# Attention by pairs of heads in one order with its neighbours, in a two-layer transformer block on one core

## The chip, the core and the metric

The kernel runs on one core of a Trainium2 chip. Its engines work side by side: TensorE (PE) multiplies into PSUM, eight banks of 512 columns; VectorE (DVE), ScalarE (ACT) and GpSimd (POOL) read and write SBUF, VectorE and ScalarE also PSUM; SyncE (SP) issues most transfers. The metric is the device time of one execution in microseconds (us). A difference is told as a per cent of the time before.

## What is computed

Four sub-layers on 2048 tokens of width 256, each with a residual and a layer norm behind it. The change touches the third (16-head causal attention, head width 16) and the seams to its neighbours:

```
x = _layernorm(x + _L0_attn_ref(x))
x = _layernorm(x + _L0_ffn_ref(x, ...))        # two experts of eight, low-rank parts
x = _layernorm(x + _L1_attn_ref(x, w_qkv, w_o))
x = _layernorm(x + _L1_ffn_ref(x, ...))        # mixture of 32 experts, top 8

# _L1_attn_ref, B = 1, S = 2048, 16 heads
q, k, v = split(x @ w_qkv.T)
scores = where(causal, q @ k.T / sqrt(16), min)
attn = softmax(scores) @ v
return attn @ w_o.T
```

## The kernel before

Every engine has its own program, written out in order; semaphores (`sig`, `sem`) join them. Tokens go in four blocks `b` (or `qb`) of 512 and 16 tiles of 128. A float32 product is made of three products of rounded parts, a high and a low one of each operand (`product`, `low`).

Attention works on four groups `g` of four heads. The queries and keys of a group stand in `stack`: per head 64 rows with the four combinations of parts, two rows for the maximum and padding up to 96 rows. Each score is computed twice. First **by query**, to find each query's maximum: a unit `(g, h, qt, kb)` is one head, one query tile and one block of keys, one product of 96 rows (L1390), on the diagonal a mask product behind it (L1393), and one VectorE reduction (L992) into `mpart`. There are 640 units; they take turns in PSUM banks 4 and 5, and a unit waits for the reduction two units back. When a round `(g, qb)` has its last unit, the maxima are reduced once more (L998), turned by TensorE (L1403), copied in two parts to `mrow` (L959, L743) and put by eight GpSimd transfers (L508) into the maximum rows of `stack`. Then **by key**: a step `(g, qb, kt)` takes one key tile against the 512 queries of the block for four heads (L1485, mask L1489), banks 0 to 3; ScalarE takes the exponentials of two heads at a time, 1024 wide (L680), and TensorE adds the values (L1447) into bank 6, for four heads in four column groups and in two halves of 256 queries. The sum of the exponentials comes with them, since the values have a column of ones. At a round's end VectorE copies bank 6 (L1027), TensorE turns it (L1503) and VectorE divides (L967, L969).

The order is set by `attention_plan`: 160 steps with 22 empty ones ahead (`lead`), and four units in every slot (`rate`). So a step's slot on TensorE holds unit, two heads, unit, two heads, unit, half of the last step's values, unit, the other half. Twelve of the empty slots are done among the queries and keys of blocks 2 and 3 (`early`). Ahead of attention stand, block by block, values, turning of the next block, queries and keys in four chunks, each written to `qk_dram` and loaded from there into `stack` by SP; GpSimd fills the padding rows (L555). In the last round's steps the output is turned and projected tile by tile for blocks 0 to 2 (`tail_turn`, `tail_tile`). Behind the last step come block 3's projection, the turning of `x` for the mixture, its logits, the gates, and then the 48 parts of the mixture, each 24 products for gates and ups and 24 for the way down.

```
lead, rate = 88, 4
steps = [None] * (lead // rate)
steps += [(g, qb, kt) for g in range(NG) for qb in range(NB) for kt in range(TPB * (qb + 1))]
return steps, [units[rate * s:rate * (s + 1)] for s in range(len(steps) + 4)], units
```

## Time and profile before

| | |
|---|---|
| median of 3 runs | 1653.36 us (1650.28 to 1655.07) |
| span of the profiled execution, first to last instruction | 1652.2 us |
| instructions in it | 22841 |

The profile gives the profiled execution as its span; no time of its own around the span is given. In its rows PE is TensorE's products, PEld its weight loads beside them. A group of instructions has its line, engine, operation, what it writes and reads, how many there are, busy time, mean time of one and the idle time of its engine ahead of it. A row of the timeline has start, length and what it is; "x3" behind it says that three were merged, and a length is then that of all. PEclk is the granted clock of TensorE, where 1.00 is 2.4 GHz and 0.50 is 1.2 GHz.

### The profile page before, as it was taken

What the parts mean: (1) busy time and instruction counts of PE and PEld (TensorE: products, weight loads), DVE (VectorE), ACT (ScalarE), POOL (GpSimd) and SP (SyncE); (2) the same over time, 40 slices, a digit from 0 to 9 for tenths busy, and PEclk for the clock granted to TensorE, in tenths of its full rate; (3) what the DMA queues carried; (4) which work ended last, traced back from release to release, by engine and by line L of the source; (5) the groups of instructions that cost most, each with busy time, mean ns of one, the idle gap of its engine ahead of it and who ended that gap; (6) DMA issues with size and microseconds to landing.
All of it is one profiled execution on the core that took longest, in us unless ns stands there. A gap on an engine that the chain in (4) does not pass through costs nothing.

```text
span 1652.2 us, 22841 instructions
## 1 busy us (share of the span) xinstructions
PE 1528.5 (93%) x9236; PEld 1130.4 (68%) x9236; DVE 998.6 (60%) x1864; ACT 616.6 (37%) x900; POOL 275.7 (17%) x282
## 2 busy tenths in 40 slices
PE   5699999999997689999999999999889999999994
PEld 4578788788786445555555555555678888888884
DVE  3555664746646666777777777773457444565444
ACT  3132422323323101455455455447423444444441
POOL 3220110200202132010011001001012222232220
PEclk9699999999999855899999999999979999999997
DMA  6000000000002558000800530100001111111110
GB/s 259 0 1 1 1 1 0 1 0 1 20 0 70 141 97 95 9 2 1 101 5 2 64 42 2 37 2 2 2 19 49 58 46 44 46 48 49 48 55 26
DMA packets 30329, 59.77 MB, mean 36 GB/s; under 512 B 7440, under 2 KB 14352, under 8 KB 28176
## 3 DMA queue, kind: packets, MB, share of 16 engines
q1 hardware_dynamic: 26128, 58.04, 16.0%
q8 instruction: 73, 1.20, 0.3%
q0 software_dynamic: 4096, 0.28, 0.3%
q14 instruction: 32, 0.26, 0.1%
HBM read 47.41 MB, written 10.49 MB: 35 GB/s over the span
## 4 chain that ended last, share of the span: by engine, by line
PE 82%; DVE 12%; ACT 2%; issue 2%; DMA 1%; POOL 0%; POOLq 0%; DVEq 0%; ACTq 0%
PE ps L1188 47%; PE ps L1390 12%; PE ps L1447 9%; PE ps L1485 8%; DVE x L762 2%; DVE mpart L992 2%; PE ps L1489 1%; PE ps L1393 1%; DMA qk_dram<-qk_out 1%; PE ps L1204 1%; PE ps L1235 1%; PE ps L1220 1%; PE ps L1503 1%; DVE ln_stats L750 1%; ACT probs L680 1%
## 5 line engine op out<-in xcount | busy, mean ns | idle before, releaser
L992 DVE TENSOR_REDUCE mpart<-ps 128x1 f32<-128x512 f32 (+3 forms) x640 | 379.9, 609 | 141.8 <-PE ps L1390 85.8
L680 ACT ACTIVATE probs<-ps 128x1024 f32<-128x1024 f32 (+3 forms) x320 | 274.9, 894 | 305.3 <-PE ps L1489 156.5
L1390 PE MATMUL ps<-stack 96*128 96x512 f32 (+3 forms) x640 | 289.8, 463 | 19.1 <-DVE mpart L992 12.4
L1188 PE MATMUL ps<-xtd,gu 128*128 128x512 f32 x1152 | 273.3, 393 | 1.5 <-issue 1.1
L1188 PEld LDWEIGHTS ps<-xtd,gu 128*128 128x128 f32 x1152 | 214.7, 190 | 45.4 <-DVE hmul L1141 1.2
L1390 PEld LDWEIGHTS ps<-stack 96*128 96x128 f32 x640 | 129.6, 204 | 148.4 <-DVE mpart L992 77.0
L1485 PE MATMUL ps<-stack 96*128 96x512 f32 (+3 forms) x640 | 204.2, 397 | 0.0
L1188 PE MATMUL ps<-ma,b 128*128 128x512 f32 x672 | 169.1, 401 | 10.3 <-DVE x2f L908 7.4
L1447 PE MATMUL ps<-probs,vaug 128*32 128x256 f32 (+1 forms) x2304 | 176.3, 385 | 0.0
L1188 PEld LDWEIGHTS ps<-ma,b 128*128 128x128 f32 x672 | 126.9, 191 | 44.2 <-DVE x2f L908 10.8
L508 POOL DMA_DIRECT2D stack<-mrow x128 | 65.9, 523 | 508.0 <-DVE mrow L743 508.0
L1188 PEld LDWEIGHTS ps<-dn,hpart 128*128 128x128 f32 x1152 | 144.4, 191 | 5.4 <-DVE hpart L743 1.9
L1188 PE MATMUL ps<-dn,hpart 128*128 128x256 f32 x1152 | 145.8, 283 | 1.5 <-DVE hpart L743 1.5
L1485 PEld LDWEIGHTS ps<-stack 96*128 96x128 f32 x640 | 123.2, 200 | 12.2 <-issue 2.1
L1141 DVE TENSOR_TENSOR hmul<-ps,silu 128x512 f32<-128x512 f32 x96 | 66.2, 689 | 99.1 <-ACT silu L718 99.0
L590 ACT ACTIVATE hpart<-hfull 128x512 fp32r<-128x512 f32 x96 | 60.7, 632 | 154.3 <-DVE hfull L1147 154.3
L908 DVE TENSOR_TENSOR x2f<-ps,silu 128x512 f32<-128x512 f32 x56 | 38.7, 691 | 130.3 <-ACT silu L635 130.3
L575 POOL TENSOR_TENSOR gu<-gu_raw,gu 128x512 fp32r<-128x512 f32 x48 | 62.0, 1291 | 308.4 <-ACT dn L590 308.4
L743 DVE TENSOR_TENSOR hpart<-hfull,hpart 128x512 fp32r<-128x512 f32 x96 | 66.5, 693 | 67.0 <-ACT hpart L590 67.0
L1188 PE MATMUL ps<-x,w2a 128*128 128x512 f32 x336 | 90.5, 406 | 0.0
L635 ACT ACTIVATE silu<-ps 128x512 f32<-128x512 f32 x56 | 33.5, 598 | 147.2 <-PE ps L1188 147.2
L1188 PE MATMUL ps<-xtb,w 128*128 128x512 f32 x336 | 85.0, 403 | 3.6 <-ACT bc_mask L590 3.6
(168 smaller groups left out, 1700.2 us busy)
## 6 DMA issues: line engine op xcount, KB each, us to landing
stack<-qk_dram SPq DMA_DIRECT2D x24, 512.0 KB
gu_raw<-in_wgu SPq DMA_DIRECT2D x48, 256.0 KB, 2.6
qk_dram<-qk_out SPq DMA_DIRECT2D x16, 512.0 KB, 3.3
dn_raw<-in_wdn SPq DMA_DIRECT2D x48, 128.0 KB, 2.7
stack<-qk_dram SPq DMA_DIRECT2D x32, 128.0 KB, 5.6
x<-in_x_tm SPq DMA_DIRECT2D x4, 512.0 KB, 5.3
xt_in<-in_x_fm SPq DMA_DIRECT2D x1, 2048.0 KB, 9.3
stack<-mrow POOLq DMA_DIRECT2D x128, 2.0 KB, 1.6
```

The lines of the kernel that those rows point to most:

```text
L508: pool.dma_start(stack[row:row + 1, g % 2, 0, h, BLK * qb:BLK * (qb + 1)].bitcast(F32) .rearrange("a (t q) -> a t q", q=P), mrow[TPB * h:T ...
L575: settle(pool.tensor_tensor(gu[:, n % 3, 1, :, :, :].rearrange("p a b c -> p (a b c)"), gu_raw[:, n % 3, :], gu[:, n % 3, 0, :, :, :].rear ...
L590: return act.activation(out, in_, ACT.Copy)
L680: act.activation(probs[:, (2 * s + p) % 4, :, off:BLK], ps[:, 2 * p:2 * p + 2, off:BLK], ACT.Exp, scale=float(HD) ** -0.5).then_inc(exp_do ...
L743: return dve.tensor_tensor(out, full, hi.bitcast(F32), ALU.subtract)
L908: dve.tensor_tensor(x2f[:, k, :], ps[:, 1, :], silu0[:, k, :], ALU.mult) \
L992: dve.tensor_reduce(mpart[:, n % 2, TPB * h + qt % TPB, kb:kb + 1], ps[:, 4 + unit_no[u] % 2, 0:width], AX_X, ALU.max).then_inc(reduced.se ...
L1141: dve.tensor_tensor(hmul[:, tb, :], ps[:, 5 + 2 * tb, :], silu1[:, tb, :], ALU.mult) \
L1188: mm = pe.matmul(out, lhs(i), rhs(k), start=first and n == 1, stop=last and n == todo, **more)
L1390: mm = pe.matmul(ps[:, 4 + n % 2, 0:width], stack[:, g % 2, 0, h, P * qt:P * (qt + 1)], stack[:, g % 2, 1, h, BLK * kb:BLK * kb + width], ...
L1447: mm = pe.matmul(ps[32 * h:32 * (h + 1), 6, lo:hi], vaug[:, v0:v0 + 32], probs[:, (2 * r + h // 2) % 4, h % 2, lo:hi], start=kt == 0 and h ...
L1485: mm = pe.matmul(ps[:, h, off:BLK], stack[:, g % 2, 1, h, P * kt:P * (kt + 1)], stack[:, g % 2, 0, h, BLK * qb + off:BLK * (qb + 1)], star ...
```

## The change

- **Pairs of heads.** The stack has three combinations of parts instead of four: 48 rows for the scores by query (`KROWS`), 50 with the two maximum rows for those by key (`STEP_ROWS`). Of two heads one stands at row 0, the other at row 64, so two products of 50 rows lie in different halves of TensorE's rows and write two banks. The padding and its fills are gone; rows of ones are set by four transfers of SP.
- **Units of a bank pair.** A unit is now a query tile and a key block for two heads, 1024 columns, with one reduction (L1094). On the diagonal, where tiles are narrower, two diagonal units, one half and two part units of a round cover four query tiles (L1097, L1100, L1104, L1105). There are 272 units instead of 640.
- **A ring.** Units, key-major products of two heads (a step has two), queries and keys, values, turnings, projections and logits are cells; cell n uses bank pair n modulo 3 and waits for the reader of the cell before in it (`slot_free`). Banks 6 and 7 keep their roles.
- **One order.** `attention_plan` returns one list from the first value product to the end of the mixture; every engine walks it and does its own part. A unit is added where the account of VectorE's time (`count["dve"]`) isn't above that of ScalarE (`count["act"]`), or where the first step of a round is due and its maxima have not been settled for three cells; units of the next group open eight steps into the group.
- The values are added in one piece of 512 queries. ScalarE copies bank 6 (it was VectorE). GpSimd puts the maximum rows with four transfers instead of eight, 1024 elements each.
- The tail of blocks 0 to 2 lies in the last two rounds by whole blocks, that of block 3 among the first mixture parts; the mixture itself keeps its products.

On TensorE, in the step phase of group 1 before the change (L1390 unit, L1485 step, L1447 values, L1393 mask):

```order
L1390 MATMUL ps<-stack 128x512
L1485 MATMUL ps<-stack 128x512 x2
L1390 MATMUL ps<-stack 128x512
L1485 MATMUL ps<-stack 128x512 x2
L1390 MATMUL ps<-stack 128x512
L1447 MATMUL ps<-probs,vaug 32x256 x4
L1390 MATMUL ps<-stack 128x256
L1393 MATMUL ps<-trimax,identb 128x128
L1447 MATMUL ps<-probs,vaug 32x256 x4
```

and after it, at the end of a round of group 2 and the start of the next one (L1560 step, L1565 its mask, L1583 values, L1506 unit, L1528 its mask, L1545 the turned maxima):

```order
L1560 MATMUL ps<-stack 128x128 x2
L1565 MATMUL ps<-triexp,identb 128x128 x2
L1583 MATMUL ps<-probs,vaug 32x256 x4
L1506 MATMUL ps<-stack 128x512 x30
L1506 MATMUL ps<-stack 128x128 x8
L1528 MATMUL ps<-trimax,identb 128x512 x2
L1506 MATMUL ps<-stack 128x128 x8
L1528 MATMUL ps<-trimax,identb 128x512 x2
L1545 MATMUL ps<-ident,nmx 16x128
L1506 MATMUL ps<-stack 128x256 x4
```

The 30 products are 15 full units in a row, with no step product among them; before, one unit stood between the products of a step's two halves, throughout.

On VectorE, over the same kind of place, before (L992 the maximum of one unit, L998 a round's last reduction, L959 and L743 the row copies, L1027 the sums, L967 and L969 the division):

```order
L992 TENSOR_REDUCE mpart<-ps 128x1 x28
L1027 COPY usum<-ps 128x512
L992 TENSOR_REDUCE mpart<-ps 128x1 x4
L967 RECIPROCAL rec_c<-ps 128x16
L969 TENSOR_TENSOR o_tm<-ps,rec_c 128x4x64
L992 TENSOR_REDUCE mpart<-ps 128x1 x16
L998 TENSOR_REDUCE nmx<-mpart 128x16
L992 TENSOR_REDUCE mpart<-ps 128x1 x4
L959 CAST mrow<-ps 16x128
```

and after (L1094 a full unit, L1097 a diagonal, L1100 a half, L1104 and L1105 a part unit, L1112 the last reduction, L1120 and L879 the row copies):

```order
L1094 TENSOR_REDUCE mpart<-ps 128x2 x15
L1112 TENSOR_REDUCE nmx<-mpart 128x16
L1097 TENSOR_REDUCE mpart<-ps 128x4x2 x2
L1100 TENSOR_REDUCE mpart<-ps 128x4
L1120 CAST mrow<-ps 16x128
L879 TENSOR_TENSOR mrow<-ps,mrow 16x128
L1104 TENSOR_REDUCE mpart<-ps 128x2
L1105 TENSOR_REDUCE mpart<-ps 128x2
L1104 TENSOR_REDUCE mpart<-ps 128x2
L1105 TENSOR_REDUCE mpart<-ps 128x2
L1094 TENSOR_REDUCE mpart<-ps 128x2
```

The sums' copy is gone from VectorE, and five kinds of reduction replace the one.

On TensorE at the end of attention, before (L1503 sums turned, L1195 turning, L1188 products: `wo,ot` projection, `wg_118,xtd` logits, `xtd,gu` mixture):

```order
L1447 MATMUL ps<-probs,vaug 32x128 x4
L1503 MATMUL ps<-ident,usum 128x128 x4
L1195 MATMUL ps<-ident,o_tm 128x128 x8
L1195 MATMUL ps<-ident,x 128x128 x8
L1188 MATMUL ps<-wo,ot 128x256 x24
L1188 MATMUL ps<-wg_118,xtd 128x32 x24
L1195 MATMUL ps<-ident,x 128x128 x16
L1188 MATMUL ps<-wg_118,xtd 128x32 x24
L1195 MATMUL ps<-ident,x 128x128 x8
L1188 MATMUL ps<-wg_118,xtd 128x32 x48
L1188 MATMUL ps<-xtd,gu 128x512 x24
```

and after:

```order
L1560 MATMUL ps<-stack 128x128 x2
L1565 MATMUL ps<-triexp,identb 128x128 x2
L1583 MATMUL ps<-probs,vaug 32x256 x4
L1308 MATMUL ps<-xtd,gu 128x512 x12
L1583 MATMUL ps<-probs,vaug 32x128 x4
L1308 MATMUL ps<-xtd,gu 128x512 x12
```

The first mixture product now stands between the last two value products; the projections, turnings and logits of blocks 0 to 2 stand ahead of it among the steps.

The core of the diff:

```
-MROW = 4 * HD
-STK = 96
+HP = GH // 2
+RING = 3
+KROWS = 3 * HD
+STEP_ROWS = KROWS + 2
...
-
-    lead, rate = 88, 4
-    steps = [None] * (lead // rate)
-    steps += [(g, qb, kt) for g in range(NG) for qb in range(NB) for kt in range(TPB * (qb + 1))]
-    units = [(g, h, qt, kb) for g in range(NG) for qb in range(NB) for h in range(GH)
-             for qt in range(TPB * qb, TPB * (qb + 1)) for kb in range(qb + 1)]
-    return steps, [units[rate * s:rate * (s + 1)] for s in range(len(steps) + 4)], units
...
+    units, closes = [], {}
+    for n, (g, qb) in enumerate(rounds):
+        mine = [("diag", g, qb, 0), ("diag", g, qb, 1), ("half", g, qb, 0), ("part", g, qb, 0), ("part", g, qb, 1)]
+        mine += [("full", g, qt, kb, p) for qt in range(TPB * qb, TPB * (qb + 1)) for kb in range(qb) for p in range(HP)]
+        units += mine
+        closes[mine[-1]] = n
...
+    def cell(kind, key, slot=None):
+        plan.append((kind, key, count["cell"] % RING if slot is None else slot))
+        count["cell"] += 1
+        for item in [i for i in later if i[0] <= count["cell"]]:
+            later.remove(item)
...
+    def unit():
+        u = units[count["unit"]]
+        count["unit"] += 1
+        cell("unit", u)
+        count["dve"] += 1.22
+        if u in closes:
+            after_cells(2, "max", closes[u])
+            after_cells(3, "maxc", closes[u])
+            count["dve"] += 1.0
...
+    def open_units(r):
+        if count["unit"] == len(units):
+            return False
+        g = units[count["unit"]][1]
+        return r >= (g - 1) * per_group + 8 if g else True
...
+    tail = [last_step[rounds.index((NG - 1, b))] for b in range(NB)]
+    for b in range(NB - 1):
+        for d, what in ((3, "turnO"), (5, "proj"), (6, "resC"), (8, "normC"), (9, "turnD"), (11, "logit")):
+            at(tail[b] + d, what, b)
+    for d, what in ((1, "rexp"), (2, "best"), (4, "share"), (6, "kept"), (8, "combine"), (11, "ce")):
+        at(tail[2] + d, what, 0)
...
+    for r, (g, qb, kt) in enumerate(steps):
+        n = rounds.index((g, qb))
+        for p in range(HP):
+            while True:
+                if kt == 0 and p == 0 and (n not in settled or count["cell"] < settled[n] + 3):
+                    if open_units(r):
+                        unit()
+                        continue
+                    if n not in settled:
+                        for item in sorted(later):
+                            mark(item[1], item[2])
+                        later.clear()
+                elif open_units(r) and count["dve"] <= count["act"]:
+                    unit()
+                    continue
+                break
+            cell("st", (r, p))
+            count["act"] += 0.2 + 0.00083 * 2 * (BLK - max(0, kt - TPB * qb) * P)
+            ended = rounds.index(steps[r - 2][:2]) if r >= 2 and r - 2 in last_step.values() else None
+            if ended is not None:
+                if p == 0:
+                    mark("ucopy", ended)
+                    count["act"] += 0.6
+                else:
+                    mark("out", ended)
+                    after_cells(1, "head", ended)
+                    count["dve"] += 0.8
+        if r:
+            mark("pv", r - 1)
...
+    end = len(rounds) - 1
+    cell("gu", (0, 0, 0), 2)
+    mark("pv", len(steps) - 1)
+    mark("ucopy", end)
...
+        held_by = {0: ("turnC", 0), 1: ("lora_rows", (NB - 1, NC - 1)), 2: ("lora_rows", (NB - 1, NC - 1)),
+                   3: ("head", last_round)}
+        before = {}
+        for kind, key, slot in plan:
+            if slot is not None:
+                before[kind, key] = held_by[slot]
+                held_by[slot] = (kind, key)
+        misc = [(kind, key) for kind, key, slot in plan if kind in ("max", "out")]
+
+        def slot_free(eng, kind, key):
+
+            held, by = before[kind, key]
+            eng.wait_ge(*released[held].after(by))
...
+            def ones_rows(i):
+                for par in range(2):
+                    lo = 64 * par + KROWS
+                    sp_.dma_start(stack[lo:lo + 2, i, 1, :, :, :].rearrange("a n i (m t) -> a (n i m) t", t=256).bitcast(F32),
+                                  ones_row[:, None, :].broadcast_to([2, HP * T // 256, 256]).bitcast(F32)) \
+                        .then_inc(ones_in[i], 16)
...
+                for m in range(2):
+                    for part, done in ((0, qk_hi), (1, qk_lo)):
+                        sp_.wait_ge(*done.after((b, m)))
+                        sp_.dma_start(qk_dram[2 * m:2 * m + 2, part, :, BLK * b:BLK * (b + 1)].rearrange("c p t -> p c t"),
+                                      qk_out[:, m, part, :, :].bitcast(F32)).then_inc(qk_out_sem[m], 16)
+                for m in range(2):
+                    sp_.wait_ge(qk_out_sem[m], 32 * (b + 1))
+                    load_block(0, m, b, first_in[b])
+            sp_.wait_ge(ones_ready, 1)
+            for i in range(2):
+                ones_rows(i)
...
+                dve.wait_ge(*scored.after(u))
+                if kind == "full":
+                    qt, kb, p = u[2:]
+                    ins = dve.tensor_reduce(mpart[:, n % 2, :, p, qt % TPB, 2 + kb], banks(slot), AX_X, ALU.max)
...
+                elif kind == "half":
+                    ins = dve.tensor_reduce(mpart[:, n % 2, :, :, 2, 0], banks(slot).rearrange("p a (i k) -> p a i k", i=HP),
...
+                ins.then_inc(reduced.sem, 1)
...
-            def score_units(s, first, last):
...
-                        pe.wait_ge(*reduced.after(units[n - 2]))
-                    mm = pe.matmul(ps[:, 4 + n % 2, 0:width], stack[:, g % 2, 0, h, P * qt:P * (qt + 1)],
-                                   stack[:, g % 2, 1, h, BLK * kb:BLK * kb + width], start=True, stop=not last)
-                    if last:
-                        mm = pe.matmul(ps[:, 4 + n % 2, width - P:width], identb[:, :], trimax[:, :],
-                                       start=False, stop=True)
-                    mm.then_inc(scored.sem, 1)
...
+            def score(out, par, g, p, b, t, kb, k0, width, first):
+
+                lo = 64 * par
+                return pe.matmul(out, stack[lo:lo + KROWS, g % 2, 0, b, p, P * t:P * (t + 1)],
+                                 stack[lo:lo + KROWS, g % 2, 1, kb, p, k0:k0 + width],
+                                 start=first, stop=True, skip_group_check=True)
...
+                slot_free(pe, "unit", u)
+                if kind == "full":
+                    qt, kb, p = u[2:]
+                    for par in range(2):
+                        mm = score(ps[:, 2 * slot + par, :], par, g, p, qt // TPB, qt % TPB, kb, 0, BLK, True)
+                elif kind == "diag":
+                    qb, i = u[2:]
+                    for n, (p, t) in enumerate([(p, 2 * i + t) for p in range(HP) for t in range(2)]):
+                        for par in range(2):
+                            score(ps[:, 2 * slot + par, P * n:P * (n + 1)], par, g, p, qb, t, qb, P * t, P, n == 0)
+                    for par in range(2):
+                        mm = pe.matmul(ps[:, 2 * slot + par, :], identb[:, :], trimax[:, None, :].broadcast_to([P, TPB, P]),
+                                       start=False, stop=True, skip_group_check=True)
...
+            def scores_by_key(r, p, slot):
+
...
+                slot_free(pe, "st", (r, p))
+                k0 = P * (kt % TPB)
+                for par in range(2):
+                    lo = 64 * par
+                    mm = pe.matmul(ps[:, 2 * slot + par, off:BLK], stack[lo:lo + STEP_ROWS, g % 2, 1, kt // TPB, p, k0:k0 + P],
+                                   stack[lo:lo + STEP_ROWS, g % 2, 0, qb, p, off:BLK],
+                                   start=True, stop=not diag, skip_group_check=True)
+                if diag:
+                    for par in range(2):
+                        mm = pe.matmul(ps[:, 2 * slot + par, off:off + P], identb[:, :], triexp[:, :], start=False, stop=True,
+                                       skip_group_check=True)
+                mm.then_inc(st_ready.sem, 1)
...
```

## Rows read from the trace of the kernel before

**Rows 1.** The page: busy time of each engine.

```profile
PE 1528.5 (93%) x9236; PEld 1130.4 (68%) x9236; DVE 998.6 (60%) x1864; ACT 616.6 (37%) x900; POOL 275.7 (17%) x282
```

**Rows 2.** Stages: busy us (count) of each engine, PEclk, DMA share, GB/s.

```profile
501.00:635.00 134.00, 100.75 (x401) 69.21 (x400) 90.21 (x146) 23.59 (x45) 37.53 (x22) 0.75 0.47 102
635.00:1152.00 517.00, 510.03 (x3837) 280.01 (x3837) 362.31 (x648) 257.55 (x302) 57.44 (x112) 0.97 0.22 27
1152.00:1235.00 83.00, 70.09 (x507) 55.16 (x505) 43.11 (x140) 32.73 (x48) 8.02 (x8) 0.86 0.03 10
```

**Rows 3.** One step: start us, length us, engine, line, count [idle <- releaser].

```profile
700.25 0.50 PE L1390 MATMUL ps<-stack 96*128 96x512 f32 x1
...
700.59 0.63 PE L1485 MATMUL ps<-stack 96*128 96x512 f32 x2
700.79 2.08 DVE L992 TENSOR_REDUCE mpart<-ps 128x1 f32<-128x512 f32 x3 [0.70 <-PE ps L1390]
...
701.05 0.40 PE L1390 MATMUL ps<-stack 96*128 96x512 f32 x1
...
701.25 1.94 ACT L680 ACTIVATE probs<-ps 128x1024 f32<-128x1024 f32 x2 [1.62 <-PE ps L1485]
...
702.06 0.64 PE L1447 MATMUL ps<-probs,vaug 128*32 128x256 f32 x8
...
702.63 0.39 PE L1390 MATMUL ps<-stack 96*128 96x256 f32 x1
...
703.59 0.50 PE L1390 MATMUL ps<-stack 96*128 96x512 f32 x1
```

**Rows 4.** Groups by form, 700 to 1104: busy us, mean ns | idle before.

```profile
L992 DVE TENSOR_REDUCE mpart<-ps 128x1 f32<-128x512 f32 x327 | 223.0, 690 | 73.9 <-PE ps L1390 53.5 <-PE ps L1393 17.6
L680 ACT ACTIVATE probs<-ps 128x1024 f32<-128x1024 f32 x162 | 157.4, 1021 | 131.1 <-PE ps L1485 109.2 <-PE ps L1489 21.9
...
L992 DVE TENSOR_REDUCE mpart<-ps 128x1 f32<-128x128 f32 x48 | 13.7, 286 | 2.9 <-PE ps L1393 2.9
...
L680 ACT ACTIVATE probs<-ps 128x256 f32<-128x256 f32 x24 | 9.2, 384 | 24.7 <-PE ps L1489 24.7
...
L959 DVE CAST mrow<-ps 16x128 fp32r<-16x128 f32 x12 | 3.3, 279 | 3.0 <-PE ps L1403 2.5
```

**Rows 5.** Timeline of a diagonal step, the first two heads.

```profile
676.50 0.40 PE L1485 MATMUL ps<-stack 96*128 96x512 f32 x1
...
677.14 0.47 PE L1390 MATMUL ps<-stack 96*128 96x512 f32 x1
```

**Rows 6.** Timeline, the maximum rows of one round.

```profile
608.76 4.10 POOL L508 DMA_DIRECT2D stack<-mrow  x8 [26.36 <-DVE mrow L743]
```

**Rows 7.** TensorE's clock: three stretches.

```profile
603.00:635.00 32.00, 27.32 (x54) 13.21 (x55) 24.84 (x44) 0.00 (x0) 17.91 (x10) 0.50 0.55 80
635.00:671.00 36.00, 35.64 (x148) 20.13 (x147) 18.90 (x33) 10.75 (x13) 4.10 (x8) 0.50 0.84 92
672.00:700.00 28.00, 27.59 (x214) 15.09 (x214) 21.60 (x37) 13.55 (x17) 0.00 (x0) 1.00 0.00 1
```

**Rows 8.** Timeline of TensorE at 0.50.

```profile
656.00 1.08 PE L1447 MATMUL ps<-probs,vaug 128*32 128x256 f32 x8
...
657.02 0.79 PE L1390 MATMUL ps<-stack 96*128 96x512 f32 x1
```

**Rows 9.** Timeline ahead of attention.

```profile
515.00 3.04 PE L1188 MATMUL ps<-b,x 128*128 128x256 f32 x24
...
529.94 14.91 DVE L762 TENSOR_SCALAR x<-x,ln_mv,ln_rstd 128x256 f32<-128x256 f32 x4 [1.12 <-POOL ln_rstd L498]
...
556.75 3.60 SPq L443 DMA_DIRECT2D stack<-qk_dram  x8
```

**Rows 10.** The page: transfers, KB each, us from issue to landing.

```profile
stack<-qk_dram SPq DMA_DIRECT2D x32, 128.0 KB, 5.6
...
stack<-mrow POOLq DMA_DIRECT2D x128, 2.0 KB, 1.6
```

1136 lines of the change are left out of this document (575 added, 561 removed).

## The prediction

> **What bounds the kernel now.** I read the page first, then the busy time by stage, then the timeline of one step, then groups by form. The page [rows 1] has TensorE busy for 93% of the span, VectorE 60%, ScalarE 37%, which looks like a kernel that any saving on TensorE will shorten. The stages [rows 2] say where: 134 us from the last block of the first expert layer to the first key-major score (501 to 635), 517 us of attention with TensorE at 510, 83 us of tail, and the 417 us of mixture that are left of the span; the first 501 us are untouched. One attention step [rows 3] runs from 700.25 to 703.59, so 3.34 us. In it VectorE does three maxima in 2.08 us and a fourth beside them, ScalarE two exponentials in 1.94 us, and TensorE is never free for long. The point to see is that all three work in the same 3.34 us: VectorE's 2.5 to 2.8 us and ScalarE's 1.94 us add up to more than the step and still fit, because each step carries four units of maxima and four heads of exponentials side by side.
>
> **Maxima, part by part.** Before, 640 reductions; a 512-wide one takes 690 ns and a 128-wide one 286 ns [rows 4], so 404 ns for 384 elements, 1.05 ns each. A 1024-wide reduction is then 690 + 512 x 1.05 = 1230 ns: two 512-wide ones cost 1380, so only 11% is saved on one. There are 272 units (192 full, 32 diagonal, 16 half, 32 part; a part is two reductions, 0.15 us more). All maxima come to 272 x 1.23 + 5 = 340 us.
>
> **Exponentials** stay as they are: 320, 1021 ns each at 1024 wide [rows 4] and 1.94 us for two in a row [rows 3]. The copy of the sums moves to ScalarE, 16 x 0.6 us.
>
> **TensorE.** A head's score product of 512 columns has 50 or 48 rows instead of 96, and two heads stand in opposite halves of the rows. Two such products now take 0.46 us (700.59 to 701.05) [rows 3]. No row shows a pair in row halves: side by side it would be 0.23, one after the other 0.46. Values: eight records 0.57 us, twice in a step [rows 3]; in one piece between 0.9 and 1.14 us. A full step's key-major work is then 2 x (0.23 to 0.46) + (0.9 to 1.14) = 1.4 to 2.1 us against ScalarE's 1.94.
>
> **The order is what decides.** Counted in the one list, the units don't alternate with the steps. After 10 units ahead of the first step and 5 single ones, all other 257 stand in 12 unbroken runs of 10, 20, 29, 18, 21, 29, 18, 21, 29, 18, 21 and 23; between them stand the steps with no unit at all. The list forces a round's units whenever its first step is due, and that puts VectorE's account so far ahead that no unit is added until the next round is due. The ring holds three cells, so neither engine can run ahead over a run: in a unit run ScalarE has nothing, in a step run VectorE has next to nothing. Work that shared 3.34 us is put end to end: per full step 1.95 us of exponentials, and 1.7 units of 1.23 us = 2.1 us, 4.05 together.
>
> - Unit runs, VectorE-bound: 257 x 1.23 + 30 x 0.15 + 15 closings x 0.76 (0.2 for the last reduction, 0.28 each for the two row copies [rows 4]) = 332 us. Diagonal units have eight short products and two masks on TensorE; at the low clock this may outlast the reduction: 0 to 25 us, I take 10. Sum 342.
> - Step runs: 96 full steps x 1.95 = 187. The 64 diagonal steps are narrower on ScalarE (0.83 ns an element by the 1024- and the 256-wide row [rows 4], so 1.94, 1.62, 1.2, 0.77 = 5.5 us a round), but the masks stay: two heads with masks take 0.64 us at 512 columns (676.50 to 677.14) [rows 5], so four heads and the values make 2.4, 1.9, 1.5 and 1.2 = 7.0 us a round on TensorE. I take 7.0, x 16 = 112. Sums copy and its turning, 16 x 0.9 = 14. Sum 313.
> - Change-overs, 12 each way: first product to first exponential 0.66 us (700.59 to 701.25) [rows 3]. The maximum rows go in four DMAs by GpSimd instead of eight (4.10 us for eight [rows 6], so 2.05, and 1.6 to land [rows 10]): 3.7 us, and three units of 1.23 stand behind them, 3.7 us. This wait is hidden, just; without those units it would cost 3.7 us each time. Taken: 15 us (0 to 30).
> - Tail and first mixture parts inside the last steps: three projections and three logits hold TensorE for 24 products each, 3.04 us for 24 [rows 9]; with ScalarE's lead of some 0.7 us gone they cost about 2.3 each = 14; six turnings 1.1 to 1.5 each = 9; weight copies and the rest 7. Sum 30 (20 to 45). The 83 us of [rows 2] go.
>
> **Clock.** In 603 to 635, where only units ran before, the granted clock was 0.50, the lower level of 1.2 GHz, and it stayed there until 671, for 36 us in which TensorE was busy 35.64; from 672 it was 1.00 [rows 7]. Unit runs of 6 to 36 us will bring it down again. VectorE hides that, but the first steps behind it don't: at the low clock eight value records took 1.02 us (656.00 to 657.02) [rows 8] instead of 0.57, and two products will take about twice 0.46 at most, so a full step is 2 x (0.43 to 0.85) + 1.9 = 2.8 to 3.6 us, 0.8 to 1.7 over ScalarE's. If it returns after two steps, 12 x 2 x 0.85 = 20 us, and 30 for diagonal steps, whose light load may drop it as well. I take 50, between 0 and the 236 us of the rival below.
>
> By the Trainium skill's "TensorE: Matmul & The Clock Gate", Part 3, matmuls in different row groups run concurrently, a few ns apart; by that a full step at the low clock would be 2.8 us, without it 3.6; no row here has row groups. The skill's page "TensorEngine Tiling (Array Packing)", section PSUM Bottleneck, says that tiling speeds up TensorE but not the emptying of PSUM, which speaks against this change. By it the sum above stands; were TensorE still the bound, a full step with its units would cost it 1.8 to 2.9 us instead of 3.34, and 96 of them 40 to 150 us less.
>
> **Before the first step.** Per block 24 value products of 256 columns 3.04 us [rows 9], 24 query/key products of 512 columns at most twice that, say 5.7, turning 1.1: 9.8, x 4 = 39 from about 507, plus 3 for the last lora product and 2.3 a block for the two copies of 1024 columns that it waits for (by the elements in [rows 4]): about 560 for the last query/key cell. A stall goes too: VectorE's four normalisations of 256 elements took 14.91 us [rows 9] beside GpSimd's fill of the padding rows, a fill that the changed kernel doesn't have. Then SP: the first step needs rows of ones, queued behind the last block's loads: writing about 3, twelve issues at 0.45 (eight in 3.60) 5.4, four more 1.8, landing 5.6 [rows 9, 10] = 16, so the first step at 577 (565 to 600). 76 us instead of 134.
>
> **Mixture** 417 us, plus block 3's tail on TensorE (3.0 twice, 1.1 twice, 8), less some 5 us, an estimate, for the middle of the mixture, where the accumulation is now read behind the next part's products: 420 (412 to 432).
>
> **Sum.** 501 + 76 + (342 + 313 + 15 + 30 + 50 = 750) + 420 = 1747 us of span. The executions' median is 1.2 us above the span of the profiled one (1653.36 and 1652.2), so 1748 us. Attention and tail go from 600 to 750, the queries and keys give back 58.
>
> **Rivals.**
> - The clock stays at 0.50 in the step runs, as it did before from 635 to 671 with TensorE nearly full. Full steps 96 x (0.85 to 1.65) = 82 to 158, diagonal rounds 16 x 4.9 = 78: 160 to 236 in place of 50, so 1858 to 1934, middle 1895. If the pairs don't run side by side, this is the likelier. Against it: 672 onwards shows that such steps can hold 1.00. Chance 0.20.
> - The clock is back at once and ScalarE hides the diagonal steps: less 50, 24 and 10: 1664. For it: the clock's mean over all of attention was 0.97 [rows 2]. Chance 0.16.
> - Pairs one after the other: a full step 2.06 instead of 1.95, 11 us, and dearer low-clock steps, 15: 1774, within the forecast's range.
> - Faster than before: the change-overs overlap. ScalarE would start while VectorE still holds two units (2.46 us), VectorE while ScalarE holds two exponentials (up to 1.9): 12 x 4.36 = 52 and the 15 above, 67. On top of the second rival: 1597. It decides from 16 us, 0.7 a change-over. Against it: the rows of the maximum need 3.7 us [rows 6, 10] and hold the first step back until the units are nearly done. Chance 0.06.
>
> **How the numbers follow.** Forecast 1748 with 0.55 (own range 1700 to 1800), the others as given, and 0.03 for a time within 0.3%, which is about what a measurement of this kernel can tell from no change. Faster 0.06, same 0.03, slower 0.91. 1655 to 1885 leaves out the fastest case and the upper half of the low-clock one, some 0.18.
>
> **What would show it.** In the profile after: ScalarE idle in stretches of 12 to 36 us between rounds while VectorE is full, and the reverse; a 1024-wide reduction near 1.23 us; a full step near 1.95 us at clock 1.00; first step near 577; attention 750 us with TensorE far below 90%. Wrong would be: VectorE and ScalarE both busy over 70% in the same slices, a reduction much below 1.2 us, or a clock of 0.50 right through the steps.

## The result and the profile after

The changed kernel takes **1753.56 us** (median of 4, 1753.27 to 1754.35), the kernel before 1651.86; the ratio is 1.0617 (95% interval 1.0602 to 1.0632). So the change makes it 6% slower. A time here is the median of all runs of a kernel and a ratio goes by its fast runs that were not profiled, so it need not be that of two medians; one run in all was slow, 1829.47 us with the kernel of two cells. The profiled execution has a span of 1752.5 us. These lines of its page answer to [rows 1]; the second group has the span in 40 slices, in tenths busy.

```profile
span 1752.5 us, 20379 instructions
...
PE 1515.7 (86%) x8212; PEld 1029.4 (59%) x8212; DVE 908.9 (52%) x1473; ACT 615.6 (35%) x884; POOL 211.1 (12%) x215
...
PE   5699999999988578887887788779688999999996
...
DVE  4555646546464453455435543572634654475444
ACT  2122323233222134432453235225262343434341
...
PEclk9799999999999567676777677678598999999998
```

No engine is the bound in the attention (slices 14 to 30 of 43.8 us each): VectorE and ScalarE go up and down against each other, and TensorE, which was busy for 510 of 517 us there [rows 2], has gaps. By stages, the windows below answer to [rows 2] (same columns): up to the first exponential, attention with the tail, mixture. The next two are a unit run and the step run behind it.

```profile
501.00:582.70 81.70, 59.30 (x335) 48.99 (x334) 40.09 (x59) 20.62 (x21) 3.54 (x6) 0.85 0.43 144
582.70:1300.80 718.10, 579.31 (x3272) 235.75 (x3272) 354.38 (x471) 283.15 (x352) 39.95 (x69) 0.71 0.13 18
1300.80:1752.50 451.70, 423.37 (x2392) 366.97 (x2388) 238.17 (x413) 166.80 (x290) 96.53 (x95) 0.97 0.14 42
...
685.50:720.30 34.80, 24.64 (x89) 10.65 (x87) 34.02 (x35) 0.00 (x0) 2.04 (x4) 0.54 0.00 1
720.80:762.90 42.10, 39.03 (x279) 13.17 (x279) 1.92 (x6) 34.07 (x42) 2.05 (x4) 0.90 0.21 27
```

In 34.8 us VectorE works for 34.02 and ScalarE for nothing; in the next 42.1 us VectorE works for 1.92. That is the order of [rows 3] taken apart. The groups (busy us, mean ns | idle before) say the same in sums; the first two answer to [rows 4].

```profile
L1094 DVE TENSOR_REDUCE mpart<-ps 128x2 f32<-128x1024 f32 x192 | 219.4, 1217 | 121.9 <-PE ps L1506 121.7
L799 ACT ACTIVATE probs<-ps 128x1024 f32<-128x1024 f32 x224 | 213.3, 1053 | 397.9 <-PE ps L1560 382.7 <-PE ps L1565 15.1
...
L1560 PE MATMUL ps<-stack 50*128 50x512 f32 x448 | 105.4, 540 | 52.9 <-DMA stack<-mrow 36.9 <-DMA stack<-ones_row 10.7 <-DVE mpart L1094 3.2
```

Now the timeline of a stretch inside a unit run, of one inside a step run, and of the change from one to the other with the round change that follows.

```profile
692.33 6.87 DVE L1094 TENSOR_REDUCE mpart<-ps 128x2 f32<-128x1024 f32 x6
692.47 0.80 PE L1506 MATMUL ps<-stack 48*128 48x512 f32 x2 [0.34 <-DVE mpart L1094]
...
693.60 0.80 PE L1506 MATMUL ps<-stack 48*128 48x512 f32 x2 [0.34 <-DVE mpart L1094]
...
668.66 8.36 ACT L799 ACTIVATE probs<-ps 128x1024 f32<-128x1024 f32 x9 [0.31 <-PE ps L1560]
...
673.48 0.73 PE L1560 MATMUL ps<-stack 50*128 50x512 f32 x4
...
674.32 1.06 PE L1583 MATMUL ps<-probs,vaug 128*32 128x512 f32 x8
...
657.30 1.20 DVE L1094 TENSOR_REDUCE mpart<-ps 128x2 f32<-128x1024 f32 x1
...
658.42 1.22 PE L1560 MATMUL ps<-stack 50*128 50x512 f32 x4 [3.09 <-DMA stack<-mrow]
659.26 2.85 ACT L799 ACTIVATE probs<-ps 128x1024 f32<-128x1024 f32 x3 [25.71 <-PE ps L1560]
...
661.99 0.62 ACT L709 ACTIVATE usum<-ps 128x512 f32<-128x512 f32 x1
662.47 1.05 ACT L799 ACTIVATE probs<-ps 128x1024 f32<-128x1024 f32 x1
...
662.66 1.11 PE L1592 MATMUL ps<-ident,usum 128*128 128x128 f32 x4 [1.28 <-ACT usum L709]
...
663.70 1.94 PE L1583 MATMUL ps<-probs,vaug 128*32 128x512 f32 x8
...
665.57 1.22 PE L1560 MATMUL ps<-stack 50*128 50x512 f32 x4
666.41 1.94 ACT L799 ACTIVATE probs<-ps 128x1024 f32<-128x1024 f32 x2 [2.89 <-PE ps L1560]
```

A unit comes every 1.13 us (693.60 less 692.47), VectorE without a gap and TensorE waiting for it. In the step run nine exponentials follow each other in 8.36 us, so a full step, two of them, is 1.83. At the change TensorE waits 3.09 us for the maximum rows, which come 0.1 us ahead of the end of the last reduction (657.30 + 1.20). The lines from 661.99 on are the surprise: ScalarE copies the old round's sums, TensorE has waited 1.28 for it, transposes them for 1.11 and does the values for 1.94, all at the low clock, and ScalarE idles 2.89.

### The profile page after: what moved, and what is told of

Same layout as the page of the kernel before. It is cut to its first block, busy times and chain, and to the rows that moved or that the text cites. A ratio compares the mean times of both kernels' runs of the same rounds, so it can differ in the third digit from the quotient of the medians.

```text
span 1752.5 us, 20379 instructions
## 1 busy us (share of the span) xinstructions
PE 1515.7 (86%) x8212; PEld 1029.4 (59%) x8212; DVE 908.9 (52%) x1473; ACT 615.6 (35%) x884; POOL 211.1 (12%) x215
## 4 chain that ended last, share of the span: by engine, by line
PE 65%; DVE 20%; ACT 6%; issue 5%; DMA 2%; POOL 1%; SPq 0%; POOLq 0%; ACTq 0%; DVEq 0%
PE ps L1308 45%; DVE mpart L1094 10%; PE ps L1583 6%; PE ps L1560 4%; ACT probs L799 3%; PE ps L1506 2%; PE ps L1565 1%; PE ps L1528 1%; DMA stack<-mrow 1%; DVE x L898 1%; DVE mpart L1100 1%; POOL stack L679 1%; PE ps L1330 1%; PE ps L1592 1%; PE ps L1361 1%
## 5 line engine op out<-in xcount | busy, mean ns | idle before, releaser
L799 ACT ACTIVATE probs<-ps 128x1024 f32<-128x1024 f32 (+3 forms) x320 | 268.1, 916 | 435.8 <-PE ps L1560 382.7
L1308 PE MATMUL ps<-xtd,gu 128*128 128x512 f32 x1152 | 283.5, 401 | 7.7 <-DVE x L1138 4.8
L1094 DVE TENSOR_REDUCE mpart<-ps 128x2 f32<-128x1024 f32 x192 | 219.4, 1217 | 121.9 <-PE ps L1506 121.7
L1506 PE MATMUL ps<-stack 48*128 48x512 f32 (+3 forms) x832 | 200.0, 562 | 71.7 <-DVE mpart L1094 60.0
L1506 PEld LDWEIGHTS ps<-stack 48*128 48x128 f32 x832 | 98.0, 275 | 189.0 <-DVE mpart L1094 132.8
L1560 PE MATMUL ps<-stack 50*128 50x512 f32 (+3 forms) x640 | 143.2, 495 | 53.1 <-DMA stack<-mrow 36.9
L1583 PE MATMUL ps<-probs,vaug 128*32 128x512 f32 (+3 forms) x1280 | 169.0, 604 | 4.9
L1560 PEld LDWEIGHTS ps<-stack 50*128 50x128 f32 x640 | 61.3, 215 | 182.9 <-ACT probs L799 76.0
L679 POOL DMA_DIRECT2D stack<-mrow x64 | 33.2, 525 | 644.0 <-DVE mrow L879 643.8
L879 DVE TENSOR_TENSOR hpart<-hfull,hpart 128x512 fp32r<-128x512 f32 x96 | 66.5, 693 | 67.0 <-ACT hpart L709 67.0
L822 ACT ACTIVATE silu<-ps 128x512 f32<-128x512 f32 x96 | 57.4, 598 | 97.9 <-PE ps L1308 94.4
```

The lines of the kernel that those rows point to most:

```text
L679: pool.dma_start(stack[row:row + 1, g % 2, 0, qb, :, :].bitcast(F32) .rearrange("a i (t q) -> a (i t) q", q=P), mrow[HP * TPB * par:HP * T ...
L799: act.activation(probs[:, (2 * r + p) % 4, :, off:BLK], banks(slot)[:, :, off:BLK], ACT.Exp, scale=float(HD) ** -0.5).then_inc(exp_done.se ...
L822: act.activation(silu1[:, tb, :], ps[:, 2 * slot, :], ACT.Silu).then_inc(silu1_ready.sem, 1)
L879: return dve.tensor_tensor(out, full, hi.bitcast(F32), ALU.subtract)
L1094: ins = dve.tensor_reduce(mpart[:, n % 2, :, p, qt % TPB, 2 + kb], banks(slot), AX_X, ALU.max)
L1308: mm = pe.matmul(out, lhs(i), rhs(k), start=first and n == 1, stop=last and n == todo, **more)
```

## The experiments

Twelve kernels, each timed against the kernel before on the same chip. "Attention" is from the first exponential to the first product of the mixture: 718.0 us in the changed kernel, and 585.5 before (637.2 to 1222.7).

**Clock in the unit runs.** Full units' products four times over:

```diff
-                    for par in range(2):
+                    for par in (0, 1) * 4:
```

> Order of the changed kernel; each full unit's pair of products is computed four times over into the same banks, so that TensorE stays busy in the unit runs (4 x 0.24 = 0.97 us of 1.13). It prices the low clock. From the trace the low clock behind a unit run costs 2.3 us in each of 12 step runs and 6 us in the first two rounds: 1720 us (1710 to 1730) with the granted clock at 1.00 in the step runs. Rival (the low clock weighs what the prediction took, 50 us, or more): 1700 or less. Third: the clock falls all the same, 1753 or a few us more.

Measured 1754.76 us (ratio 1.0626), attention 717.5. The time is that of the third outcome, the cause another: the granted clock of the unit runs is 1.00 now, but from 719.2 to 729.4 it is 0.50, that is from the run's last units, which aren't repeated, through TensorE's wait of 2.7 us for the maximum rows into the first steps. The twelve unit runs got 5.8 us shorter, 304.2 for 310.0: in the changed kernel VectorE waits 6.4 us in them for the diagonal units' products, which the low clock stretches, and here not at all. The repeated products gave that back: the gaps from the last exponential to a run's first reduction grew by 6 us. So the low clock in the unit runs costs some 6 us, and its price in the steps stayed open.

**VectorE in the unit runs.** A full unit's reduction reads half its columns (half the maximum is left out).

```diff
-ins = dve.tensor_reduce(mpart[:, n % 2, :, p, qt % TPB, 2 + kb], banks(slot), AX_X, ALU.max)
+ins = dve.tensor_reduce(mpart[:, n % 2, :, p, qt % TPB, 2 + kb], banks(slot)[:, :, 0:256], AX_X, ALU.max)
```

> Order of the changed kernel; the 192 full units reduce only 256 of each bank's 512 columns, so half the maximum is left out. It prices VectorE in the unit runs. Serial theory with VectorE as the end of each unit: a reduction of 512 elements takes 0.6 us at close spacing in place of 1.13, 192 x 0.53 = 102 us less: 1651 us (1640 to 1680). Rival (TensorE at the low clock, two products 0.8 us and the hand-over, is right behind VectorE): a unit stays at 0.8 to 1.0 us and the gain is 25 to 60 us, 1695 to 1728.

Measured 1666.06 us (1.0086), attention 635.1, so 83 us less.

```profile
L1094 DVE TENSOR_REDUCE mpart<-ps 128x2 f32<-128x512 f32 x192 | 116.9, 681 | 122.2 <-PE ps L1506 122.2
...
677.09 13.24 DVE L1094 TENSOR_REDUCE mpart<-ps 128x2 f32<-128x512 f32 x22 [21.10 <-PE ps L1506]
```

Busy time falls from 219.4 to 116.9, by 102.5, and 83 of them come off the span: VectorE's work in the unit runs lies on the path. The second row answers to the rival, TensorE right behind VectorE: 22 reductions in 13.24 us are one every 0.60 us where it was 1.13, so in full units VectorE is still the end and the rival fell. The twelve unit runs went from 310.0 to 220.3 us, 90 less. Of the 13 missing there to 102.5, 9 are VectorE's waits for the diagonal units' products, up from 6.4 to 15.5 us; another 7 went outside the runs, above all where the maximum rows, no longer hidden behind slow reductions, come later than the units' end (the gap at round 1 grew from 6.25 to 10.86).

**The order, units spread evenly.** Ring, cells and products as they were, but for the emptying of a projection cell, which moves two cells behind it. The limit at `open_units` stays.

```diff
+    def due(r):
+        return 10 + 2.7 * min(r, 24) + 1.75 * max(r - 24, 0)
...
-                elif open_units(r) and count["dve"] <= count["act"]:
+                elif open_units(r) and count["unit"] < due(r + p / HP):
```

> Same cells, same ring of three, but the 257 late units are spread evenly among the steps: 2.7 units a step up to step 24, 1.75 a step after it, none in the last 23 steps (the emptying of a projection cell is moved to two cells behind it). Serial theory (the 12 unbroken unit runs put VectorE's 310 us and ScalarE's step runs end to end): up to step 24 VectorE decides, 2.7 x 1.13 = 3.05 us a step, 76 us with the closings; 113 steps at about 2.15 (1.75 units x 1.13 = 1.98, and TensorE 1.8 + 1.75 x 0.25), 243; the last 23 steps 45; round changes 24; tail 30: 418 in place of 718, so about 1452 us (1420 to 1520), faster than the kernel before. ScalarE and VectorE both over 60% busy in the same slices. Rival A (three cells are too few for two engines to overlap, whatever the order): 1650 to 1750. Rival B (TensorE or its clock is the limit): the clock stays at 0.50 as the units stand among steps, 1700 or more.

Measured 1624.44 us (0.9861, 0.9805 to 0.9917), attention 577.6. 129 us come from the order, and the kernel is 1.4% faster than the one before; but 300 were expected. (The profiled execution is the fastest of four, 1612.4 us, so 577.6 is on the low side.) The timeline of one step with two units:

```profile
940.11 0.50 PE L1565 MATMUL ps<-stack 50*128 50x512 f32 x2 [0.85 <-DVE mpart L1099]
...
940.54 1.06 PE L1588 MATMUL ps<-probs,vaug 128*32 128x512 f32 x8
...
941.54 0.50 PE L1511 MATMUL ps<-stack 48*128 48x512 f32 x2
...
942.09 2.36 DVE L1099 TENSOR_REDUCE mpart<-ps 128x2 f32<-128x1024 f32 x2 [0.89 <-PE ps L1511]
...
942.32 1.02 ACT L804 ACTIVATE probs<-ps 128x1024 f32<-128x1024 f32 x1 [0.64 <-PE ps L1565]
...
943.37 0.50 PE L1565 MATMUL ps<-stack 50*128 50x512 f32 x2 [0.86 <-DVE mpart L1099]
```

The step takes 3.26 us (943.37 less 940.11), and in it each of the three engines has a wait: with three cells, TensorE waits for VectorE to free one (0.86), and VectorE waits 0.89 while the values product stands ahead of its next unit. From step 24 on, 42 full steps have two units, a round's second step left out; from exponential to exponential their median is 3.31. The 18 with one unit have 2.10. I had counted 2.15 for 1.75 units. Call this the ring theory: a step's length is set by the waits for a free cell, not by the engines' own work.

**Half of the units spread.** One unit a step (0.9), the rest ahead of the round.

```diff
-                elif open_units(r) and count["dve"] <= count["act"]:
+                elif open_units(r) and count["unit"] < base[0] + 0.9 * (r + p / HP - base[1]):
```

> One unit for each step is put among the steps, the rest of a round's units stays in a run ahead of its first step: 135 of the 257 are interleaved, 122 stay in runs of 10 to 17. Serial theory: an interleaved unit is hidden behind ScalarE's 1.83 us, 135 x 1.13 = 153 us gained, less some 20 for TensorE in the diagonal steps: about 1620 us (1590 to 1650). If the gain of the even order came from something else than the number of units in runs (the end of the clock's falls, the change-overs), this kernel would give little, 1700 or more, as its 11 change-overs stay.

Measured 1652.12 us (1.0001), attention 611.8: 106 us less, of 135 units' 153. The first unit of a step is thus mostly hidden (a full step with one has a median of 2.12 us here, 1.83 without) and gives most of the gain; the further units of the even order gave only 34 us more, 28 by the medians.

**Two cells instead of three**, on the even order: `RING = 2`.

> As e1_even with a ring of two cells in place of three (and the emptying of a projection cell one cell behind it). Ring theory: each handing over of a cell now stands in the path, a full step with two units goes from 3.25 to about 3.9 us, attention gets 115 us longer and the stage of q/k/v 10: about 1745 us (1710 to 1780). Rival (the engines' own work bounds e1_even, not the number of cells): under 1650.

Measured 1808.24 us (1.088), attention 770.7, so 193 more, where 115 were expected. That the number of cells sets the time is shown, and its price was put too low: with two cells the even order is worse than the serial one with three. Part of the price may be the clock, which is at 0.50 for 481 us of the attention here and for 170 in the even order; no run splits it.

**The values product moved into the wait.** First as a whole cycle of four steps (`s` a cell of two heads, `U` a unit, `.` the last step's values):

```diff
+        order = ("sU.sU", "sUsU.", "sUs.", "sUs.U")
+        return order[r % 4] if count["unit"] < len(units) else "ss."
```

> As e1_even, but the cells of the steps stand in a fixed cycle of four steps with seven units, in which the values product of a step stands where TensorE otherwise waits for VectorE: (s, U, values, s, U), (s, U, s, U, values), (s, U, s, values), (s, U, s, values, U), with s a cell of two heads' key-major scores and U a unit; the same cycle from the first step on, so the first two blocks of a group still get short runs. In e1_even a full step with two units took 3.25 us and one with one unit 1.9. Ring theory (with three cells a cell comes free only when its reader is done, and the values product of 1.0 us in TensorE's order then lies between the free cell and its filling): the same units in this cycle take about 2.4 us a full step in place of 2.9 on the mean of four, 40 us less for the attention: about 1580 us (1565 to 1600). Rival (TensorE's throughput or its clock bounds e1_even): the cycle holds the same products and gives nothing, 1615 to 1630.

Measured 1601.66 us (0.9705), attention 563.9: 14 less than the even order in the profiled runs, 23 by the medians, of 40 expected. Then alone, on the even order:

```diff
+            if p and r and middle:
+                mark("pv", r - 1)
```

> e1_even with one move: from step 24 on, in every step with two units the values product stands behind the second unit and ahead of the second key-major cell, in place of behind both. In e1_even such a step takes 3.25 us, 32 full ones and 21 diagonal ones: TensorE waits 0.85 us for VectorE to free a cell, then fills it and does the values product for 1.0 us while VectorE has nothing left. Ring theory (the values product can stand in that wait): 3.25 goes to about 2.8 us, attention 577.6 to about 560. Rival (the engines' own work fills such a step): it stays at 3.1 to 3.3 us and attention within 5 us.

Measured 1622.41 us (0.9811), attention 581.1. From exponential to exponential, the 42 full steps with two units went from a median of 3.31 to 3.05, as the ring theory wants, but the 18 with one unit went from 2.10 to 2.57 and the second step of a round from 5.16 to 6.30. At that step the cause can be read:

```profile
940.47 1.94 PE L1594 MATMUL ps<-probs,vaug 128*32 128x512 f32 x8 [1.18 <-ACT usum L720]
...
943.17 1.02 ACT L810 ACTIVATE probs<-ps 128x1024 f32<-128x1024 f32 x1 [2.85 <-PE ps L1571]
```

The values product now stands ahead of the round's second pair of heads and waits 1.18 us for ScalarE's copy of the old sums; with its own 1.94 us at the low clock it holds up the next scores, and ScalarE idles 2.85. The clock was at 0.50 for 197 us of the attention, 170 before. So the local gain was given back; why the clock is low for longer, and what that costs, is open.

**The round change.** ScalarE's copy of the sums right behind the first step of the new round:

```diff
-                if p == 0:
-                    mark("ucopy", ended)
...
+            if r - 1 in last_step.values():
+                mark("ucopy", rounds.index(steps[r - 1][:2]))
```

> Order of the changed kernel; only ScalarE's copy of a finished round's sums moves: from behind the first exponential of the new round's second step to behind the new round's first step, two exponentials earlier relative to the transposes that need it. It prices the round change. In the changed kernel a round's second step takes 5.2 us in place of 1.86, fifteen times, 50 us: TensorE waits 1.2 us for the copy, then does the four transposes (1.1) and the values (1.9 at the low clock) before the next scores, and ScalarE idles 2.7. Theory (the wait for the copy is the head of that chain): 1.2 to 1.9 us less at each of 15, 20 to 28 us: 1728 us (1722 to 1736). Rival (the transposes and values at the low clock alone fill it, the wait is covered): under 8 us, 1746 or more.

Measured 1732.23 us (1.0482), attention 696.5, 21.5 less, as expected. The same change as above, at round 7; ScalarE's last wait is 1.24 us where the changed kernel has 2.68 at this place:

```profile
888.98 1.12 PE L1592 MATMUL ps<-ident,usum 128*128 128x128 f32 x4
...
890.03 1.44 PE L1583 MATMUL ps<-probs,vaug 128*32 128x512 f32 x8
...
891.94 6.52 ACT L799 ACTIVATE probs<-ps 128x1024 f32<-128x1024 f32 x7 [1.24 <-PE ps L1560]
```

**Clock in the steps.** Products repeated in all units but the diagonal ones, and 14 pairs ahead of a round's first wait.

```diff
+                if (kt, p) == (0, 0) and r:
+                    slot_free(pe, "st", (r, p))
+                    for par in (0, 1) * 14:
+                        score(ps[:, 2 * slot + par, :], par, g, 0, qb, 0, 0, 0, BLK, True)
```

> Order of the changed kernel with products repeated so that TensorE stays busy up to and across each change from units to steps: full units four times, half and part units three times, and 14 pairs of products into the first cell of a round ahead of its wait for the rows of the maximum. It prices the low clock of the step runs, which e3_busy left as it was. From the changed kernel's trace: a round change at the low clock takes 7.7 us, at the full clock 5.4, 12 x 2.3 = 28 us, and some 6 in the first two rounds: 1720 us (1712 to 1732) if the clock is 1.00 at the first steps of the runs. Prediction's term: 50 us less, 1703. Third: the clock falls all the same, 1750 to 1760.

Measured 1768.83 us (1.0696), attention 729.9. None of the expectations: the clock did rise, and the time too. Windows over rounds 7 to 11 and over the first two steps of round 6; first this kernel, then the changed one.

```profile
899.00:1110.00 211.00, 197.78 (x1529) 97.94 (x1528) 85.41 (x102) 96.68 (x120) 10.23 (x20) 0.98 0.14 16
...
838.80:844.40 5.60, 3.68 (x30) 1.41 (x28) 0.68 (x2) 4.34 (x6) 0.00 (x0) 1.00 0.00 0
```
```profile
892.60:1100.00 207.40, 172.16 (x1008) 64.14 (x1007) 85.69 (x102) 97.48 (x120) 10.24 (x20) 0.74 0.14 16
...
831.60:838.70 7.10, 5.82 (x30) 2.05 (x28) 0.68 (x2) 4.34 (x6) 0.00 (x0) 0.53 0.01 2
```

At 0.98 instead of 0.74 the five rounds take 3.6 us more. The repeated products cost more than they bring: over the attention the gaps between unit and step runs grow from 31 to 46 us, so the total says nothing on the clock's price. The second pair of rows does: the same thirty products with the same exponentials take 5.6 us at 1.00 and 7.1 at 0.53. From a round's first exponential to that of its third step, rounds 6 and 10 take 5.52 us here and 6.99 and 7.15 in the changed kernel. Of the ten rounds behind a unit run and without tail work they are the only two that had no low clock at all; the others take 6.7 to 7.2 us. The run also speaks against the clock as what the spread order gained: low clock for 73 us of the attention instead of 419, and no gain.

**Both ends of the attention.** SP writes the rows of ones ahead of block 3's queries and keys, and block 3's tail is spread over parts 3 to 10.

```diff
+                if b == NB - 1:
+                    sp_.wait_ge(ones_ready, 1)
+                    for i in range(2):
+                        ones_rows(i)
...
+    extra = {(3, 0): ("turnO", NB - 1), (4, 0): ("proj", NB - 1), (4, 1): ("resC", NB - 1), (5, 1): ("normC", NB - 1),
```

> The order of the changed kernel in the attention, with two moves at its ends. SP writes the rows of ones ahead of the last block's queries and keys; and the last block's tail (turning, projection, residual, normalisation, logits) is spread over parts 3 to 10 of the mixture, in place of parts 0 to 7. Theory: the first step waits for the rows of ones and nothing else, so it comes some 8 us earlier, at 575; the first ten mixture parts, 25 us longer than ten steady ones of which 8 are TensorE's own work, lose the two waits of 4.2 and 4.8 us and the low clock behind them, some 12 us. Sum 1733 us (1728 to 1742). Rivals: the first step is held by the rows of the maximum or the block's keys right behind (0 to 2 us from there), and the mixture's waits come back at the new places (1750).

Measured 1741.48 us (1.0534): 12 of 20. The first exponential comes at 573.8 instead of 582.7, 8.9 earlier; the mixture is 444.8 instead of 451.8, 7 of 12; the attention took 2.4 more.

**Together.** Cycle and ends, then these with the earlier copy of the sums.

> The cycle of e5_cycle with both moves of e7_ends. If the three parts are separate, their gains add: 1580 less 20, about 1560 us (1540 to 1585), some 5% under the kernel before. If the attention in the cycle is slowed by the earlier rows of ones or the mixture's order, 1580 or more.

Measured 1585.09 us (0.9598, 0.9576 to 0.9619).

> e8_best with the earlier copy of the sums of e9_sums. In e8_best a round's second step takes 5.8 us in place of some 2.5: 15 times 1 to 1.9 us less, 15 to 28: about 1563 us (1555 to 1575), 5.4% under the kernel before. If in the interleaved order another wait takes the copy's place, 1580 or more.

Measured 1579.69 us (0.9587, 0.9537 to 0.9637): 10% under the changed kernel and 4% under the one before, but the last step gave 5 us of 20, within the two intervals. The page of the last one, to be held against the first fence:

```profile
DVE  3555754664755456778877677663344754574545
ACT  3032332422322233436665466445634334433441
...
573.80:1126.90 553.10, 506.05 (x3276) 214.05 (x3276) 366.67 (x473) 294.65 (x352) 39.84 (x69) 0.83 0.18 24
```

VectorE and ScalarE are now high in the same slices, 6 to 8 and 3 to 6 tenths, so neither is the bound. TensorE is busy for 506 of the attention's 553 us at a mean clock of 0.83 (last row), where the changed kernel had 579 of 718: how far it has become the bound again was not tried.

## Why the prediction was right

The time came out 6 us above the 1748 predicted, and the mechanism is the one named: the list puts unit runs and step runs end to end. The spread order took 129 us off with the same work, and the narrowed reduction 83. That it came so close is luck: the attention was put 32 us too long and the mixture 32 too short, and inside the attention several terms cancel.

| term | predicted | measured |
|---|---|---|
| first step | 577 | 582.7 |
| unit runs | 342 | 310 |
| full steps, 96 | 187 | 174 (1.81 each) |
| diagonal steps, 16 rounds | 112 | 116 (12 x 7.01, to the last exponential ahead of a unit run, and 4 x 7.85) |
| round changes | 14 | 26 (12 x 1.9 and 3 x 1.05, as at clock 1.00) |
| low clock in steps | 50 | 21 (12 x 1.74) |
| tail, and what is left | 30 | 40 (718 less the others) |
| change-overs | 15 | 31 |
| attention with tail | 750 | 718 |
| mixture | 420 | 452 |

The row of the tail is a remainder: it also holds the first round with its single units and what the low clock costs in other steps, so it doesn't test the forecast of 30.

**Unit runs.** 257 x 1.23 was wrong in its period, not in its duration: the row has 1217 ns, as worked out from [rows 4], but the next reduction starts 1.13 us after the last, so a tenth of a microsecond overlaps: 26 of the 32 us. The 10 us for diagonal units at the low clock measured 6.4. The same holds for ScalarE, whose 1021 ns of [rows 4] are 0.90 to 0.92 in a row of exponentials. [rows 3] has this already: two exponentials in 1.94. The Trainium skill has both. "Vector Engine (DVE) Microarchitecture Reference", section 5.2, gives 1.04 ns a column and some 75 ns an instruction once they queue, by which an estimate for 1024 columns is 1142 ns; "ScalarE: Activation LUTs", section "What ACT_TABLE_LOAD costs", says that back-to-back activations overlap by some 93 ns. The traces agree, with 1130 ns and with 1021 less 900 to 920.

**Round changes and clock.** I had 64 us for the two, and they are about 47, in the other proportion. Two steady full steps take 3.62 to 3.65 us, the first two of a round at clock 1.00 take 5.52, so 1.9 more, and behind a unit run, mostly at 0.50, 7.26 on the mean of ten, so 1.74 more again; the 5.52 rests on the two rounds above. At rounds 4, 8 and 12, which follow steps directly, two diagonal steps take 5.41 instead of 4.36. I had taken 0.9 from the length of the copy and its turning alone and not seen that the copy stands behind an exponential and holds up values and next scores. The run with the earlier copy shows it is this chain.

**Change-overs.** "Hidden, just" held to 0.1 us: 22 of the 24 gaps are 0.6 to 1.8 us. The other two are 6.25 and 5.74. At the last round no unit stands behind the maximum, as the list shows and as I had overlooked. At round 1 the four transfers of the rows were issued from 605.7 on and landed 6.3 to 7.0 us later, the last at 614.3, where the same transfers take 1.6 us in most rounds: in that stretch the DMA engines are 97% busy while group 1 is loaded.

```profile
595.90:615.20 19.30, 9.59 (x45) 4.88 (x43) 12.29 (x15) 0.04 (x1) 2.05 (x4) 0.50 0.97 155
...
606.45 1.54 POOL L679 DMA_DIRECT2D stack<-mrow  x3 [0.26 <-issue]
614.32 0.50 PEld L1560 LDWEIGHTS ps<-stack 50*128 50x128 f32 x4 [9.09 <-DMA stack<-mrow]
```

**Pairs.** Two heads' products are side by side: four take 0.73 us and two 0.50, so a further pair costs 0.23, the lower end. The Trainium skill's "TensorE: Matmul & The Clock Gate", Part 3, by which matmuls in different row groups run concurrently, is borne out. So is the sentence of the Trainium skill's "TensorEngine Tiling (Array Packing)", section PSUM Bottleneck, that tiling speeds up TensorE but not the emptying of PSUM: both run kinds wait for VectorE or ScalarE, and the saving on TensorE became idle time.

**Before the first step.** The rows of ones decide, as the first wait shows; the normalisation's stall is gone (1.37 us at L898 where it was 14.91 [rows 9]). That 577 and 582.7 are near is in part luck too: VectorE's last copy of queries and keys ends at 570.3, 10 us later than I had for the last cell, and from there it is 12.4 us to the first exponential, where I had 16.

```profile
581.57 0.79 PE L1560 MATMUL ps<-stack 50*128 50x512 f32 x2 [10.67 <-DMA stack<-ones_row]
```

**Mixture.** This step failed. 12 us are my boundary: the stage of 417 in [rows 2] begins at 1235, but the kernel before has its first mixture product at 1222.7, so its mixture is 429.5. The measured mixture is 22 us above those 429.5, where I had 3. The first ten parts take 109.8 us instead of 84.9, 25 more where I had 8 of TensorE's work. Two waits make up 9 of it:

```profile
PE ps L1308 <- DVE x L1138: 4.8, 1, 4.8
...
PE ps L1315 <- DVE o_tm L1130: 4.2, 1, 4.2
```

and the clock falls to 0.50 at each. A part in the middle takes 8.46 us instead of 8.34, and from the tenth part on all that makes 2.9 us (313.9 for 311.0 to the last part's first product); the stretch from the last part's first product to the end is 5.5 us shorter. Why a middle part is longer was not tried.

**Rivals.** "The clock stays at 0.50" fell: from 667.6 on it is 1.00 in that step run, though over the attention it was 0.50 for 419 of 718 us. "The change-overs overlap" fell: the maximum rows let the first product of the steps start 0.1 us ahead of the end of the last reduction, and no more. "The clock is back at once" fell: the low clock costs 1.74 us at each of 12 rounds, and the diagonal rounds take 7.0 us and more, not the 5.5 of ScalarE's work. "Pairs one after the other" fell by the pairs above.

## What to carry to other kernels

When one list sets the order of several engines, write out where each engine's items stand in it before adding up busy times: items in unbroken runs add, they don't overlap. Cells twice as wide in the same memory are half as many, and two readers on one ring need more cells than one: here a full step took 1.83 us with no unit, 2.1 with one and 3.3 with two, so three cells hid most of the first unit's 1.13 us and nothing of the second's. Price a round change by its whole chain, the engine that waits and what stands behind it in its order, not by the new instruction's length.

## What was not expected of the hardware

- The clock, held at 1.00 through a unit run by repeated products, was 0.50 at nearly each change-over all the same, for 10.2 us, in which TensorE first had little to do in the last units, then waited 2.7 us for the maximum rows and then did the first steps. With products across that wait most of the low stretches shrank to 3.4 us, and at rounds 6 and 10 there was none.
- The third cell is worth 193 us of attention here (577.6 against 770.7, with the clock lower for longer), more than the whole slowdown of the change.
- The small transfers of the maximum rows (4 KB, 1.6 us to land in most rounds) took over 6 us at round 1, while large ones had the DMA engines at 97%. The kernel before has it worse, though its steps did not wait for them: its 2 KB transfers, 1.6 us in the median, took 15 to 25 us in the rounds at 798 and 936, where the loads of the next group fill the DMA engines.
